# Gated recurrence and mixture of experts on one core: the clearing of the held rows in five transfers, and the shared down weights' loads at earlier slots

## The reference

```
k = layernorm(x);  v = ctx                                   # per channel, over the 256 steps:
y_t = (e1*aa + e2*v_t) / (e1*bb + e2)                        # a decayed running sum of exp(k)*v over exp(k)
x   = x + tanh(g_xattn) * y
h   = layernorm(x)
routed = for each token the 2 best of 8 experts (capacity 1280 rows each):
         w * ((silu(h Wg_e) * (h Wu_e)) Wd_e),  Wg_e, Wu_e 512x352, Wd_e 352x512
shared = (silu(h Sg) * (h Su)) Sd,              Sg, Su 512x1408,    Sd 1408x512
out = x + tanh(g_ffn) * (routed + shared)
```

## Time and profile before

| what | value |
|---|---|
| median of 3 timed runs | 1225.95 us (1223.76 to 1226.49) |
| profiled execution, its own time | 1231.09 us |
| its span, first to last instruction | 1229.3 us |
| mean granted TensorE clock | 0.988 of full speed |
| TensorE matmul busy | 1153.9 us (94%) |
| VectorE / GpSimd / ScalarE busy | 705.1 / 632.7 / 489.3 us |
| SP's hardware queue | 276960 packets, 112.24 MB, 40.3% of 16 engines |
| clearing of `moe_d` | 1 transfer of 2560 KB |
| shared down weights | 11 transfers of 256 KB |

### The profile page before, as it was taken

How to read it: one execution, slowest core, us unless ns; L and a number is a source line. 1 busy time by engine, 2 the same in 40 slices (tenths; PEclk the granted TensorE clock), 3 DMA queues, 4 the chain that set the end, 5 groups by cost and what they waited for, 6 DMA issues and landing times.

```text
span 1229.3 us, 26044 instructions
## 1 busy us (share of the span) xinstructions
PE 1153.9 (94%) x8284; PEld 805.0 (65%) x8284; DVE 705.1 (57%) x1385; ACT 489.3 (40%) x901; POOL 632.7 (51%) x754
## 2 busy tenths in 40 slices
PE   1487999999999999999999989999999999999998
PEld 1375777777777777777777767566666666666653
DVE  5776887787787787787887866222232222222112
ACT  5664453353353343443444344233333333333220
POOL 7886557357457456456457543344444444444320
PEclk9987999999999999999999989999999999999999
DMA  8465334333343333343443323989999999998739
GB/s 233 105 173 140 86 67 93 90 72 91 84 88 75 80 86 81 74 91 80 102 100 71 61 64 65 213 170 180 171 170 174 175 171 165 180 163 135 127 52 318
DMA packets 295942, 150.98 MB, mean 123 GB/s; under 512 B 236061, under 2 KB 260661, under 8 KB 295712
## 3 DMA queue, kind: packets, MB, share of 16 engines
q1 hardware_dynamic: 276960, 112.24, 40.3%
q0 software_dynamic: 18048, 37.47, 17.4%
q10 hardware_dynamic: 832, 0.02, 0.0%
HBM read 77.17 MB, written 52.31 MB: 105 GB/s over the span
## 4 chain that ended last, share of the span: by engine, by line
PE 82%; DVE 6%; issue 3%; DMA 2%; ACT 1%; POOL 1%; SPq 1%; DVEq 0%; POOLq 0%; ACTq 0%
PE PU L1074 30%; PE PU L1182 16%; PE PD L1107 13%; PE PD L1203 11%; PE PL L1182 5%; PE PR L1193 2%; DMA xT<-wkv 1%; PE PR L1217 1%; PE PT L1217 1%; PE PD L1217 1%; DVE wkv L1332 1%; PE PT L998 1%; DVE wkv L1349 1%; DVE srng L1367 1%; DMA k_d<-wkv 0%
## 5 line engine op out<-in xcount | busy, mean ns | idle before, releaser
L1074 PE MATMUL PU<-xT,wreg 128*128 128x256 f16 x4224 | 506.2, 276 | 3.5 <-DVE srng L1367 1.7
L1074 PEld LDWEIGHTS PU<-xT,wreg 128*128 128x128 f16 x4224 | 415.5, 99 | 85.2 <-issue 4.6
L803 POOL DMA_INDIRECT moe_d<-wkv,acc x71 | 112.1, 1578 | 216.8 <-ACT wkv L978 214.4
L1182 PE MATMUL PU<-acc,wkv 128*128 x1284 | 214.5, 312 | 0.0
L1107 PE MATMUL PD<-wreg,hreg 128*128 128x512 f16 x858 | 206.5, 379 | 0.3 <-issue 0.3
L1182 PEld LDWEIGHTS PU<-acc,wkv 128*128 128x128 f16 x1284 | 125.2, 98 | 69.3
L1604 DVE TENSOR_TENSOR wkv<-PR,wkv 128x384 f16<-128x384 f32 x71 | 39.6, 558 | 208.0 <-ACT wkv L972 154.5
L884 ACT ACTIVATE srng<-PU 128x256 f32<-128x256 f32 x176 | 66.9, 380 | 216.5 <-PE PU L1074 188.7
L1203 PE MATMUL PD<-acc,wkv 128*128 (+1 forms) x639 | 149.6, 379 | 1.5 <-DVE wkv L1604 1.5
L684 POOL TENSOR_TENSOR hreg<-srng,hreg 128x256 f16<-128x256 f32 x165 | 119.4, 728 | 43.2 <-ACT hreg L900 42.3
L1107 PEld LDWEIGHTS PD<-wreg,hreg 128*128 128x128 f16 x858 | 83.8, 98 | 74.1 <-issue 0.9
(11 more groups left out here) (178 smaller groups left out, 1340.4 us busy)
## 6 DMA issues: line engine op xcount, KB each, us to landing
wreg<-in_L_ffn_w_up_gate SPq DMA_DIRECT2D x48, 176.0 KB
acc<-in_x SPq DMA_DIRECT2D x32, 256.0 KB, 3.3
xhl_d<-wkv SPq DMA_DIRECT2D x32, 256.0 KB, 2.4
wkv<-in_ctx SPq DMA_DIRECT2D x112, 64.0 KB, 2.5
k_d<-wkv SPq DMA_DIRECT2D x28, 256.0 KB
wkv<-k_d SPq DMA_DIRECT2D x112, 64.0 KB
moe_d<-acc SPq DMA_DIRECT2D x13, 512.0 KB
out<-moe_d SPq DMA_DIRECT2D x2, 3328.0 KB, 21.0
```

The lines of the kernel that those rows point to most:

```text
L803: pool.indirect_dma_start(out=moe_d, out_offset=bass.IndirectOffsetOnAxis(ap=didx[:, t:t + 1], axis=0), in_=ostage[t % 3], in_offset=None, ...
L1074: mm = pe.matmul(PU[r][:, gu * UN:(gu + 1) * UN], sU[:, m, gu, a, kt, :], xT[:, u.par, b, kt, :], start=(kt == 0 and a + b == 0), stop=(kt ...
L1182: mm = pe.matmul(up_set[t % 2][gu][:, 0:I], xgT[:, t % 4, a, kt, :], weights(h, ((gu * 2 + b) * KT + kt) * I, P, I), start=(kt == 0 and a ...
```

## The change

The one clearing transfer of slot (0, 7) becomes five transfers of 256 rows (512 KB) each, issued at the end of slots (1, 1), (1, 4), (1, 5), (1, 6) and (1, 9). The 11 loads of down weights are issued at the end of slots (-1, 9), (0, 0) and (0, 1), where they were in (0, 3), (0, 4) and (0, 5). The counts that are waited for on `moe_started` grow by four. Nothing else differs; the bytes cleared are the same.

```diff
-D_LOAD_AT = {(0, 3): range(0, 4), (0, 4): range(4, 8), (0, 5): range(8, JT)}
+D_LOAD_AT = {(-1, 9): range(0, 4), (0, 0): range(4, 8), (0, 1): range(8, JT)}
+ZERO_AT = {(1, 1): 0, (1, 4): 1, (1, 5): 2, (1, 6): 3, (1, 9): 4}
...
-        MOE_PARTS = FIRST_HELD + 1
-        EARLY_PARTS = 11
+        MOE_PARTS = FIRST_HELD + len(ZERO_AT)
+        EARLY_PARTS = 10 + len(ZERO_AT)
+        assert (HTILES + 4) * P == len(ZERO_AT) * UN
...
+            def clear_rows(n):
+                lo = NTOK - HTILES * P + n * UN
+                sp.wait_ge(pmade, PMADE)
+                sp.dma_start(moe_d[lo:lo + UN, :].rearrange("(p a) (b c) -> p (a b) c", p=P, c=P),
+                             zeros[:, :].unsqueeze(1).to_broadcast([P, UT * KT, P])).then_inc(moe_started, 16)
...
-                    if key(u, s) == (0, 7):
-                        sp.wait_ge(pmade, PMADE)
-                        sp.dma_start(moe_d[NTOK - HTILES * P:NTOK + 4 * P, :].rearrange("(p a) (b c) -> p (a b) c", p=P, c=P),
-                                     zeros[:, :].unsqueeze(1).to_broadcast([P, (HTILES + 4) * KT, P])).then_inc(moe_started, 16)
+                    if key(u, s) in ZERO_AT:
+                        clear_rows(ZERO_AT[key(u, s)])
```

## The result

The changed kernel took 1217.79 us in the median of 6 runs (1217.21 to 1219.16), the kernel before 1225.55 us (1223.76 to 1226.49, 6 runs beside them). The ratio is 0.994, with a 95% interval of 0.9927 to 0.9952: faster by 5.9 to 8.9 us, in the median by 7.8. The forecast was 1219.0 us, with a range of 1215 to 1223.5.

A forecast was written before the change was run, and what follows sets the result against it. TensorE bounds it, waiting 10.2 us at the logits of (0, 10) for a transposition behind the clearing. Gain 9.4 - 2.5 = 6.9 us: 1231.09 to 1224.2 profiled, 1219.0 us timed; range 1215 to 1223.5.

The forecast's parts named there:

- What fills the wait: Logits of (0, 10): transposition queued behind the 2560 KB clearing, whose drain adds 8.6 us to its ordinary 3.16 us.
- The clearing's place: Slot (0, 7) without the clearing: transposition issued at 88.2, landing about 91.35; the 10.23 us wait becomes about 0.2.
- What is late next: `turn_y` in (1, 0): TensorE waits 2.7 us for the division ending at 98.61; gain up to there 9.4 us.
- The clock: After the new 2.7 us wait ahead of `turn_y` in (1, 0): clock falls to 0.50, costing 2.5 us.
- The deadline in (1, 5): `turn_y` there: result at 118.7, TensorE at 120.1 with slow clock, costing nothing; at 117.6 otherwise, costing about 1.1 us.
- the clock holds: Rival: clock stays up through the new wait ahead of `turn_y` in (1, 0); gain 8.3 us, 1217.7; chance 0.18.
- The loads in the lead-in: Down weights moved to (-1, 9), (0, 0), (0, 1): k in at 63.5, VectorE waits 0.4 us; cost 0.
- What their going frees: Slots (0, 3) to (0, 5) without loads: VectorE's 2.63 us wait for k at 86.03 goes; gain 0.
- The five clearings: Unit 1: each part 0.6 us of SP and 1.7 us of queue, 3.1 us to spare for k; cost 0.

The follow-up runs named there:

- the kernel that fills that wait: Changed kernel plus 20 unread matmuls ahead of `turn_y` in (1, 0) and 30 in the wait of (0, 5): 1217.09 us (ratio 0.9933).
- the kernel that held it: Changed kernel plus 20 matmuls of 256 columns, result unread, in TensorE's wait ahead of `turn_y` in (1, 0): 1218.93 us (ratio 0.9941).

## Why the prediction was right

The time came out as forecast and most of the steps did, but how close the numbers lie is luck in part. The working starts from one profiled execution of the kernel before, 5 us slower than the timed ones, with a wait of 10.23 us; the second profile has 8.21 us. The mechanism is the same in both, the size is not: the 7.66 us below are against the first profile, and against the second they are 5.06.

*What fills the wait.* Right. The clearing was taken to drain in 8.6 us at 305 GB/s; a window in the middle of the wait, in the first profile of before, has

```profile
94.00:96.00 2.00, 0.00 (x0) 0.00 (x0) 2.00 (x1) 1.97 (x4) 2.00 (x3) 0.50 1.02 291
```

which makes 9.0 us. And the logits follow the clearing's issue by 12.5 to 12.7 us in three executions (82.17, 86.83 and 88.88).

*The clearing's place.* Right. The transposition went out at 88.20 as forecast. The wait there became 0, not 0.2, because TensorE came later, at 92.08 and not at 91.18: the wait of (0, 5) was 3.73 us and not 2.45, and the clock stayed down until 82 to 84 us, so the 111 matmuls took 14.61 us in place of 13.49. This had an effect of 0.2 us at most, as the kernel that fills that wait shows.

*What is late next.* Right in place and size. The division ended at 97.23 + 1.40 = 98.63 (98.61 forecast), `turn_y` ran at 98.68 (98.7), TensorE waited 2.48 us (2.7). This term turned 10.2 us of removed wait into 9.4 us.

*The clock.* Right that it falls, 0.7 us too dear: the price was taken as 2.5 us from the wait before, and was 5.11 - 30 x 0.109 = 1.84 us. This is nearly the whole distance between the forecast of 6.9 us and the 7.66 against the first profile.

*The deadline in (1, 5).* Right: division at 118.7 forecast, 118.62 measured; with the slow clock TensorE came after it, with the clock held it waited 0.84 us. The rival "the clock holds" had been priced at 8.3 us; the kernel that held it reached 126.99 - 118.57 = 8.4 against the same profile.

*The loads in the lead-in.* Right: k stored at 58.4 forecast, the loads went out at 57.81; VectorE waited 0.47 us (0.4), SP was free at 67.55 (67.6).

*What their going frees.* Here the working was incomplete. It said that the loads' going gains nothing, and looked only at VectorE's wait for k. That holds beside the other half. Taken alone it is wrong: the loads alone bring nearly the whole gain, since in SP's order the clearing itself came forward by 6.7 us against the first profile of before, 4.7 against the second. The step that I left out was to ask when the old clearing would have been issued with the loads gone.

*The five clearings.* Right that they are hidden: doubled, or in one piece, or in front of a k store, they cost TensorE no wait that the trace shows. The margin was named wrongly (3.1 us for a part, where parts take about 4 to land).

One thing stays open, and the two profiles of before differ by it: why the wait of (0, 5) was 2.45 and 0.83 us in them and 3.7 us in those of the changed kernel and of either half of it. TensorE reached it earlier in the latter, since 15 matmuls at 56.8 us took 1.80 us where they took 3.01 and 3.10 at 57.2. Whether the change has a part in that was not tried. In the changed kernel the wait costs 0.2 us at most, as the kernel that fills it shows. In the kernel before, the execution with the shorter wait issued its clearing 2 us earlier.

## What to carry to other kernels

A bulk transfer that nobody waits for can be paid for by the next small transfer in its queue, so look at what is issued within its drain time, not at who reads it. Two edits that each remove the same wait do not add: work out each alone, with the new issue times of everything behind it in the queue. And when a long wait goes, list the deadlines behind it with their times, since the first that is later than the engine's new arrival, here a division at 98.6 us, sets the gain. Before a forecast is added up from one profile, compare that execution with the timed runs: here a second profile moved the size of the wait by 2 us.

## What was not expected of the hardware

The clearing of 2560 KB held up SP itself, not only the data behind it. A transposition issued in 1.27 us otherwise took 8.85 us to issue behind it, and a k store 7.91 us in place of 0.33. A transposition that came 6 us after the clearing took 3.72 us, and SP was done with it 9.7 us after the clearing's issue, as in both profiles of before (9.6 and 9.7). Whether the bytes or their runs of 512 bytes do this was not tried. Whatever else SP had to do in that time waited as well; in these kernels that was little.

Waits of similar length were followed by slow stretches of different length. In the kernel before it was about 7 us after 2.45 us of idle. In the changed one it was about 10 us after 3.73 us in the first profile (0.50 until 82 us) and about 7 us after 3.76 in the second, and 3 to 4 us after the 2.48 us ahead of 98.68. So the idle time before does not tell the length, and a price taken from one stretch was good to 0.7 us only.
